# Gathering each block of 256 edges once instead of once for each tile that it touches, in two stages of a graph network on one Trainium2 core

## What is computed

```python
x = x + L0_gnn(layernorm(x), src, dst, ...)         # GIN: sum over neighbours, then a two-layer MLP, batch norm
x = x + L0_ffn(layernorm(x)[None], ...)[0]          # mixture of 16 experts, the best 2 of them
x = x + L1_gnn(layernorm(x), node_vec1, src, dst, edge_attr_4, edge_attr_8, ...)   # tensor-product messages
x = x + L1_ffn(layernorm(x)[None], ...)[0]          # mixture of 8 experts, the best 1
```

```python
neigh = segment_sum(node_feats[src], dst)                       # L0_gnn
h = (1 + eps) * node_feats + neigh
# L1_gnn: y0 (64 values) and y1 (64 x 3) of each node; w_a..w_d (64 each) and ea0, ea1 (1 + 3) of each edge
mid0 = w_a * y0[src] * ea0
mid1 = w_b * einsum('euc,ec->eu', y1[src], ea1) / sqrt(3)
mid2 = (w_c * y0[src])[:, :, None] * ea1[:, None, :]
mid3 = (w_d * ea0)[:, :, None] * y1[src]
agg = segment_sum(concat(mid0, mid1, mid2, mid3), dst)
```

## Time and profile before

| what | us |
|---|---|
| median of three runs | 2367.6 |
| profiled execution, device time | 2366.55 |
| its span | 2364.5 |
| first gather stage, first to last gather issued | 62.7 to 641.7 |
| message stage, first to last gather issued | 1246.1 to 1891.7 |
| granted TensorE clock, mean share | 0.908 |

### The profile page before, as it was taken

How to read it: one execution, slowest core, us unless ns; L and a number is a source line. 1 busy time by engine, 2 the same in 40 slices (tenths; PEclk the granted TensorE clock), 3 DMA queues, 4 the chain that set the end, 5 groups by cost and what they waited for, 6 DMA issues and landing times. The chain is left out here.

```text
span 2364.5 us, 37045 instructions
## 1 busy us (share of the span) xinstructions
PE 1939.7 (82%) x10646; PEld 1596.8 (68%) x10646; DVE 1135.9 (48%) x2491; ACT 1031.6 (44%) x3208; POOL 1152.2 (49%) x1143
## 2 busy tenths in 40 slices
PE   2788888888688767999466988888888878959998
PEld 1555555555356647999345978878778875649997
DVE  5433333333322664444557877777777742141111
ACT  3444444444034402332265766666666626513332
POOL 1777777777600005555107777777777700002221
PEclk7899999999689558999677999999999998959999
DMA  9667676676300118999716766666666604036663
GB/s 237 182 219 223 211 224 222 212 223 211 107 18 0 55 39 293 352 353 343 194 44 198 205 185 194 190 190 189 188 189 190 176 21 92 22 107 200 199 200 98
DMA packets 273478, 413.50 MB, mean 175 GB/s; under 512 B 67662, under 2 KB 162500, under 8 KB 273053
## 3 DMA queue, kind: packets, MB, share of 16 engines
q1 hardware_dynamic: 218056, 258.46, 35.7%
q0 software_dynamic: 54784, 150.16, 21.4%
q10 hardware_dynamic: 462, 2.76, 0.4%
HBM read 324.41 MB, written 87.84 MB: 174 GB/s over the span
## 5 line engine op out<-in xcount | busy, mean ns | idle before, releaser
L1725 POOL DMA_INDIRECT msg_got<-y_dram,pair_src x464 | 505.5, 1090 | 241.8 <-issue 132.5
L1738 ACT ACTIVATE msg_scaled<-msg_plain,msg_w 128x125 f32<-128x125 f32 x1392 | 415.9, 386 | 234.5 <-DVE msg_plain L1774 224.2
L632 POOL DMA_INDIRECT sum_got<-xn_dram,pair_src x464 | 438.9, 946 | 156.1 <-issue 131.6
L673 PEld LDWEIGHTS sum_ps_sum<-sum_got,sum_onehot 128*125 128x125 f32 x928 | 178.9, 200 | 239.7 <-issue 198.7
L673 PE MATMUL sum_ps_sum<-sum_got,sum_onehot 128*125 128x256 f32 x928 | 262.3, 408 | 92.4 <-DMA sum_got<-xn_dram,pair_src 91.9
L1248 ACT ACTIVATE ffn_run_hid<-ffn_run_ps_h,cols 128x128 f32<-128x128 f32 x512 | 145.9, 368 | 391.0 <-PE ffn_run_ps_h L1207 391.0
L1756 PE MATMUL msg_ps_z<-msg_prod,msg_plain 128*125 128x256 f32 x928 | 244.4, 386 | 83.7 <-ACT msg_scaled L1738 41.0
L1765 PEld LDWEIGHTS msg_ps_z<-msg_prod,msg_scaled 128*125 128x125 f32 x2320 | 290.0, 188 | 13.2
L1765 PE MATMUL msg_ps_z<-msg_prod,msg_scaled 128*125 128x128 f32 x2320 | 291.4, 273 | 0.0
L732 DVE TENSOR_TENSOR agg<-sum_ps_sum,agg 125x256 f32 x232 | 98.5, 425 | 373.4 <-PE sum_ps_sum L673 373.4
L703 ACT ACTIVATE sum_wide<-sum_ps_w,sum_rec 128x128 f32<-128x128 f32 x416 | 130.0, 364 | 285.5 <-PE sum_ps_w L659 285.5
(11 more groups left out here) (294 smaller groups left out, 2409.8 us busy)
## 6 DMA issues: line engine op xcount, KB each, us to landing
ffn_run_w<-in_L_ffn_w SPq DMA_DIRECT2D x128, 512.0 KB, 6.6
msg_w<-edge_w SPq DMA_DIRECT2D x232, 260.0 KB
edge_w<-sum_wide SPq DMA_DIRECT2D x52, 1040.0 KB, 4.9
ffn_run_w<-in_L_ffn_Wd SPq DMA_DIRECT2D x32, 1024.0 KB, 5.6
sum_got<-xn_dram,pair_src POOLq DMA_INDIRECT x464, 3.0
msg_got<-y_dram,pair_src POOLq DMA_INDIRECT x464
ffn_rows<-xn SPq DMA_DIRECT2D x10, 560.0 KB
table_got<-ffn_results SPq DMA_DIRECT2D x10, 560.0 KB
```

What stands on the lines that cost most here:

```text
L632: pool.indirect_dma_start(got[:, n % RING, u, :], None, k.xn_dram, bass.IndirectOffsetOnAxis(ap=k.pair_src[:, n, u:u + 1].bitcast(U32), ax ...
L673: last = pe.matmul(ps_sum[n % ZB][0:P, :], onehot[n % OB][:, u, :], got[:, n % RING, u, :], start=(u == 0), stop=(u == KC - 1))
L1725: pool.indirect_dma_start(got[:, s % RS, c, :, :].rearrange("p k v -> p (k v)"), None, k.y_dram, bass.IndirectOffsetOnAxis(ap=k.pair_src[: ...
L1738: last = act.activation(scaled[s % MB][:, x, c, :], plain[s % MB][:, c, :], ACT.Copy, scale=w[:, s % RS, c, D + x:D + x + 1])
```

## The change

`prepare` no longer makes `pair_src` (the src numbers of each pair) and `pair_start`, but `block_src` (those of each block, by a plain transposition) and `pair_need`: the pair's block plus 1. Both stages gather each block once, into a ring of RING = 32 blocks, block b into place (b + 1) % 32. POOL counts the blocks that have arrived in one semaphore, `blocks_in`: LAG = 4 blocks behind the issue, it waits for the block's gathers and increments it. The readers load `pair_need` into a register, wait until `blocks_in` reaches it, and read `got` at the place need % 32. POOL waits, before it issues block b, until the pairs up to b - 8 are done (AHEAD = 32 - 25 = 7). In the message stage the ring of weights has 3 steps instead of 4, the products are made for each pair apart (six instructions of half the size), and the last two of a pair's eight output components are opened by a product of a bf16 row of ones with a bf16 row of zeros instead of by the zeros in `prod`.

```diff
@@ prepare, PE @@
-            for f, w in enumerate((1, 0)):
-                for u in range(KC):
-                    for h, (at, n) in enumerate(HALVES):
-                        last = pe.matmul(ps_two[f][:, u, :], ends_f[h][0:n, :, u, w], chosen[0:n, h, :], start=(h == 0), stop=(h == 1))
-                last.then_inc(field_ready, 1)
+            for h, (at, n) in enumerate(HALVES):
+                for u in range(KC):
+                    last = pe.matmul(ps_block[:, u, at:at + n], ends_f[h][0:n, :, u, 1], k.ident[0:n, 0:n], start=True, stop=True)
+            last.then_inc(blocks_ready, 1)
...
@@ sum_neighbours, POOL @@
-            for n in range(NPAIR):
-                if n >= RING:
-                    pool.wait_ge(summed, n - RING + 1)
+            def arrived(b):
+                pool.wait_ge(got_in[b % RING], (b // RING + 1) * 16 * KC)
+                pool.sem_inc(blocks_in, 1)
+
+            for b in range(NB):
+                if b > AHEAD:
+                    pool.wait_ge(summed, b - AHEAD)
                 for u in range(KC):
                     pool.indirect_dma_start(
-                        got[:, n % RING, u, :], None, k.xn_dram,
+                        got[:, (b + 1) % RING, u, :], None, k.xn_dram,
...
+                if b >= LAG:
+                    arrived(b - LAG)
+            for b in range(NB - LAG, NB):
+                arrived(b)
@@ sum_neighbours, PE @@
+                need = pe.value_load(k.pair_need[0:1, n:n + 1], min_val=1, max_val=NB)
+                pe.wait_ge(blocks_in, need)
                 pe.wait_ge(masked, n + 1)
-                pe.wait_ge(got_in[n % RING], (n // RING + 1) * 16 * KC)
                 for u in range(KC):
-                    last = pe.matmul(ps_sum[n % ZB][0:P, :], onehot[n % OB][:, u, :], got[:, n % RING, u, :],
+                    last = pe.matmul(ps_sum[n % ZB][0:P, :], onehot[n % OB][:, u, :],
+                                     got[:, ds(need % RING, 1), u, :].rearrange("p o d -> p (o d)"),
@@ sum_messages, POOL (the rest as in sum_neighbours) @@
+                if b > AHEAD:
+                    pool.wait_ge(made, (b - AHEAD + 1) // 2)
@@ sum_messages, PE @@
                         pe.matmul(z[0:P, 0:4, :], mask[:, c, :], p[:, c, 0:4, :], start=(u == 0), stop=False)
+                        if u == 0:
+                            pe.matmul(z[0:P, 6:8, :].rearrange("p k v -> p (k v)"), k.ones[0:1, 0:P], zeros[0:1, :], start=False, stop=False)
                     for x in range(3):
                         for u in range(KC):
                             c = KC * h + u
-                            if x == 0 and u == 0:
-                                last = pe.matmul(z[0:P, 4:8, :].rearrange("p (o k) v -> p o k v", o=2), by[:, x, c, :],
-                                                 p[:, c, 4:12, :].rearrange("p (o k) v -> p o k v", o=2)[:, :, 0:4:3, :],
-                                                 start=False, stop=False)
-                            else:
-                                last = pe.matmul(z[0:P, 4:6 + x:1 + x, :], by[:, x, c, :], p[:, c, 4 + x:8:3 - x, :],
-                                                 start=False, stop=(x == 2 and u == KC - 1))
+                            last = pe.matmul(z[0:P, 4:6 + x:1 + x, :], by[:, x, c, :], p[:, c, 4 + x:8:3 - x, :],
+                                             start=False, stop=(x == 2 and u == KC - 1))
@@ sum_messages, DVE @@
+                need = [dve.value_load(k.pair_need[0:1, n:n + 1], min_val=1, max_val=NB) for n in (2 * s, 2 * s + 1)]
                 dve.wait_ge(w_in[s % RS], 32 * (s // RS + 1))
-                dve.wait_ge(got_in[s % RS], 64 * (s // RS + 1))
-                if s >= 2:
-                    dve.wait_ge(summed, s - 1)
-                dve.tensor_tensor(p[:, :, 0:8:7, :], v[:, :, 0:4:3, :], y[:, :, 0:1, :].to_broadcast([128, CH, 2, MUL]), ALU.mult)
...
+                dve.wait_ge(blocks_in, need[1])
+                if s >= XB:
+                    dve.wait_ge(summed, s - XB + 1)
+                for h in range(2):
+                    y = got[:, ds(need[h] % RING, 1), :, :, :].rearrange("p o u k v -> p (o u) k v")
+                    at = slice(KC * h, KC * h + KC)
+                    dve.tensor_tensor(p[:, at, 0:8:7, :], v[:, at, 0:4:3, :], y[:, :, 0:1, :].to_broadcast([128, KC, 2, MUL]), ALU.mult)
+                    for q in (1, 2):
+                        last = dve.tensor_tensor(p[:, at, 3 * q - 2:3 * q + 1, :], v[:, at, q:q + 1, :].to_broadcast([128, KC, 3, MUL]),
+                                                 y[:, :, 1:4, :], ALU.mult)
+                last.then_inc(made, 1)
...
-                dve.memset(prod[b][:, :, 8:12, :], 0.0).then_inc(zeroed, 1)
+            dve.memset(zeros[:, :], 0.0).then_inc(zeros_made, 1)
```

More of the change, by code:

```diff
@@ L386, in _ @@
             last.then_inc(rows_ready, 1)
-            pe.wait_ge(chosen_made, 2)
-            pe.wait_ge(ends_made, 2)
-            for f, w in enumerate((1, 0)):
-                for u in range(KC):
-                    for h, (at, n) in enumerate(HALVES):
-                        last = pe.matmul(ps_two[f][:, u, :], ends_f[h][0:n, :, u, w], chosen[0:n, h, :], start=(h == 0), stop=(h == 1))
-                last.then_inc(field_ready, 1)
+            pe.wait_ge(ends_made, 2)
+            for h, (at, n) in enumerate(HALVES):
+                for u in range(KC):
+                    last = pe.matmul(ps_block[:, u, at:at + n], ends_f[h][0:n, :, u, 1], k.ident[0:n, 0:n], start=True, stop=True)
+            last.then_inc(blocks_ready, 1)
+            pe.wait_ge(chosen_made, 2)
+            for u in range(KC):
+                for h, (at, n) in enumerate(HALVES):
+                    last = pe.matmul(ps_two[1][:, u, :], ends_f[h][0:n, :, u, 0], chosen[0:n, h, :], start=(h == 0), stop=(h == 1))
+            last.then_inc(field_ready, 1)
             pe.wait_ge(loaded, 16 * vec_loads)
@@ L1694, in sum_messages @@
         w = ph.sb("w", [128, RS, CH, WREC])
-        got = ph.sb("got", [128, RS, CH, 4, MUL])
+        got = ph.sb("got", [128, RING, KC, 4, MUL])
         plain = [ph.sb(f"plain{b}", [128, CH, P]) for b in range(MB)]
         scaled = [ph.sb(f"scaled{b}", [128, 3, CH, P]) for b in range(MB)]
-        prod = [ph.sb(f"prod{b}", [128, CH, 12, MUL]) for b in range(2)]
+        prod = [ph.sb(f"prod{b}", [128, CH, 8, MUL]) for b in range(XB)]
         ps_z = [ph.ps(f"z{b}", [128, 8, MUL]) for b in range(ZB)]
+        zeros, zeros_made = ph.sb("zeros", [1, 2 * MUL], BF16), ph.sem("zeros_made")
         ps_lanes, lanes_made = ph.ps("lanes", [128, P]), ph.sem("lanes_made")
-        w_in, got_in = ph.sems("w_in", RS), ph.sems("got_in", RS)
-        masked, scaled_made, made, summed, added, zeroed = (
-            ph.sem(x) for x in ("masked", "scaled_made", "made", "summed", "added", "zeroed"))
+        w_in, got_in, blocks_in = ph.sems("w_in", RS), ph.sems("got_in", RING), ph.sem("blocks_in")
+        masked, scaled_made, made, summed, added = (
+            ph.sem(x) for x in ("masked", "scaled_made", "made", "summed", "added"))
         block = ph.ctx.enter_context(nc.Block())
@@ L1713, in _, with arrived @@
                     n = 2 * s + h
[L1714 removed]
+                    need = sp.value_load(k.pair_need[0:1, n:n + 1], min_val=1, max_val=NB)
                     sp.dma_start(w[:, s % RS, KC * h:KC * h + KC, :].rearrange("p u w -> p (u w)"),
[L1716 removed]
+                                 k.edge_w[ds((need - 1) * SB, SB), :].rearrange("(p u) w -> p (u w)", u=KC)).then_inc(w_in[s % RS], 16)
         @block.gpsimd
         def _(pool):
[L1720 to L1724, removed]
[L1725 to L1727 removed]
+            def arrived(b):
+                pool.wait_ge(got_in[b % RING], (b // RING + 1) * 16 * KC)
+                pool.sem_inc(blocks_in, 1)
+            for b in range(NB):
+                if b > AHEAD:
+                    pool.wait_ge(made, (b - AHEAD + 1) // 2)
+                for u in range(KC):
+                    pool.indirect_dma_start(
+                        got[:, (b + 1) % RING, u, :, :].rearrange("p k v -> p (k v)"), None, k.y_dram,
+                        bass.IndirectOffsetOnAxis(ap=k.block_src[:, b, u:u + 1].bitcast(U32), axis=0)).then_inc(got_in[b % RING], 16)
+                if b >= LAG:
+                    arrived(b - LAG)
+            for b in range(NB - LAG, NB):
+                arrived(b)
         @block.scalar
@@ L1800, in _ @@
             mask(0)
-            for b in range(2):
-                dve.memset(prod[b][:, :, 8:12, :], 0.0).then_inc(zeroed, 1)
+            dve.memset(zeros[:, :], 0.0).then_inc(zeros_made, 1)
             dve.memset(k.agg[:, :, :], 0.0).then_inc(added, 1)
```

36 lines of the change are left out of this document (20 added, 16 removed).

## The result

The changed kernel's median is 2268.96 us (four runs, 2266.26 to 2271.19), and 2366.5 us (four runs, 2364.76 to 2368.01) that of the kernel before beside it: a ratio of 0.9587, with a 95% interval of 0.9572 to 0.9602. The forecast was 2250 us with a range of 2228 to 2294. Sign and range were right, and the middle was 19 us low. The profiled execution took 2271.19 us, 95.4 less than that of before.

The account below looks back on a forecast made before the run. It took POOL to bound both gather stages, with DVE bounding the message stage after the change. 2366.55 less 60 (first stage) and 57 (message stage) gave 2249.6, so 2250 us, range 2228 to 2294.

Parts of the forecast that it names:

- The engine that holds the message stage: Message stage: DVE sets the step at 4.98 us, with PE at 4.58 and POOL at 5.06 at worst.
- First stage, 60.0 from POOL: First gather stage: 48 of 464 gathers go, 1.2505 us each, taking 60.0 us from POOL.
- `LAG` at 0: POOL's added wait and increment cost 0, since its sequencer hands over some twelve gathers ahead.
- Rival (c): POOL's sequencer instruction stands in the gather chain, 17 us in the first stage and 10 in the other: 2275; chance 0.08.
- PE's register load: First gather stage: about 1 us of sequencer a pair, hidden behind 1.73 us of products already queued.
- Rival (d): First gather stage: PE's register load empties its queue, 3.2 us a pair, 134 us slower there: 2444; chance 0.05.
- DVE's step of 4.98: Message stage: 4.35 us plus 0.20 for six products instead of three plus 0.42 of exposed register loads.
- PE's zero product at 0.11: Message stage: the added zero product costs one 128-column instruction, 0.11 us, between bounds of 0.05 and 0.48.
- rival (b): Message stage: DVE's exposure at 0.8 or PE's zero product at 0.48, a step of 5.35 us: 2293; chance 0.12.
- The 4 us kept for the first tile: Message stage: 4 us left for the first tile, where DVE still follows POOL, lowering the gain from 60.7 to 57.
- The signs: If right: 416 gathers a stage, first-stage last at about 582 us, DVE steps of 4.9 to 5.1, POOL idling.
- Rival (a): Message stage: POOL stays the bound with its stretching at 35 to 67 us: 2225 to 2256, middle 2238; chance 0.18.

Follow-up runs that it names:

- loads_early: The changed kernel with DVE's register loads for the next message-stage step moved behind this step's products: 2266.61 us, ratio 0.9574.
- z_bf16_rows128: The changed kernel with the message stage's bf16 zero product over 128 rows instead of one: 2257.68 us, ratio 0.953.
- lag1_first_stage: The changed kernel with LAG = 1 instead of 4 in the first gather stage: 2381.01 us, ratio 1.0064.
- first_stage_only: The kernel before with the changed first gather stage alone, its message stage left as it was: 2308.54 us, ratio 0.9762.
- rows128_early: The changed kernel with the bf16 zero product over 128 rows and DVE's next-step register loads behind the products: 2205.5 us, ratio 0.9329.

## Why the prediction was right, and where its size was off

- **The engine that holds the message stage: wrong.** The forecast had the stage follow DVE at 4.98 us, with PE 0.40 below. In the changed kernel PE is busy without a gap and DVE has slack (loads_early: no gain from taking work off DVE); DVE bounds only once PE's zero product is cheap (z_bf16_rows128). That the time still came out in the range was partly luck: PE's 5.13 happened to lie close above DVE's 4.98.
- **First stage, 60.0 from POOL: right** (59.9). POOL was the bound, 416 gathers 1.25 us apart. What I missed is that a sequencer which waits for the last landing also starts its drain late: 2.8 us. I had written that the stage's end keeps its shape.
- **`LAG` at 0: right**, for the reason given; lag1_first_stage showed the cover by taking it away. Rival (c) falls: "issue" stands at 0.30 us a gather as before.
- **PE's register load: hidden, as taken.** In the loop it runs 305 ns (median), not the 493 of the earlier trace rows, and 44.2 of the 46.3 us that PE waited before these products are put down to gathers. Rival (d) falls.
- **The Trainium skill's floor of about 600 ns** under a register load ("DMA: Bandwidth & Descriptors", "Latency and other measured facts") does not agree here: 305 ns on PE, and the exposed part of DVE's two is 0.31 us (z_bf16_rows128).
- **DVE's step of 4.98: right for DVE**, 5.05 where it bounds (z_bf16_rows128), with the products 0.98 us behind the mask where I had 0.59 + 0.42.
- **PE's zero product at 0.11: the mis-sized term.** It was taken as one 128-column instruction, and measures 0.10 with 128 rows, but 0.39 with its one row. PE's step was thus 5.13 and not 4.58, above DVE's 4.98. The step came out at 5.14: 115 x 0.16 = 18 us. My bounds (0.05 and 0.48) held it, and rival (b) names the place and the sign, a zero product of 0.4 us; I had priced it at its end (a step of 5.35, 2293) and gave it 0.12. Since PE's 4.58 lay only 0.40 under the bound and the term counts twice, anything over 0.31 would have made PE the bound, well inside the two ends.
- **The 4 us kept for the first tile** were hardly needed: 41.6 gained instead of 57 is 15, not 18, less.
- **The signs:** 416 gathers, the last at 582 us, the gap before the products and POOL's idle time came as written. The step of 5.14 is just over the 4.9 to 5.1.
- **Rival (a), POOL the bound: falls.** Its stretching shrank to 12.8 us, less than the 35 to 67 that I left it. That shorter products (0.42 and 0.55 us) let a gather go on sooner is argued, not shown: with the same products it was 7.4 us in z_bf16_rows128 and 22.3 in rows128_early, so how DVE and POOL fall together counts too.

The sum against the profiled execution: forecast 2249.6, plus 15 (PE's zero product, less the first tile), plus 4 (routing stage), plus 3 (drain) is 2271.6; measured 2271.2.

## What to carry to other kernels

When the forecast step of the second engine lies within a doubtful term of the first one's, price that term by the nearest row that is like it in *every* respect, rows of weights included: the row of the one-row product was the nearest, though in fp32 and without neighbours, and I passed it over for a 128-row one. Here a small product between products over 128 rows was cheaper when it was padded to their row count than over one row or 64. And where two edits each give nothing or little, run them together before dropping either: two engines may be holding the same step.

## What the runs showed of the hardware

- A product over one row or 64 rows between products over 128 rows costs 0.39 us (bf16), over 128 rows 0.10; in fp32 over one row 0.60, as it is two instructions. With one or 64 rows PEld sits idle 0.34 us before the load (77.8 us in 232), the load starts no earlier than its product, and the products ahead and behind take 0.10 and 0.11 us more; over 128 rows the load starts 0.21 us before its product. The same break shows between 128 and 32 rows (0.57 us of idle time on PEld), none between 128 and 80 or 72 rows (L396, L1039 of the changed kernel). Under bf16 over 128 rows the change of data type can cost at most the 0.05 us that the products behind it take longer (0.48 for 0.43).
- POOL's drain took 8.56 us where it began after the last landing (the changed kernel, and first_stage_only again); begun under running gathers it ended 8.9 us after the last of them had started. Why it takes 8.56 us stays open.
- POOL's gathers were stretched by 66.6 us in all beside DVE's two-input products of 512 and 768 columns, and by 12.8 with 256 and 384. The Trainium skill ("SBUF — State Buffer", "Who interferes with whom") says that a DVE instruction with two SBUF inputs contends with a GpSimd instruction that reads SBUF. The trace agrees; the size did not follow the products' length alone, as 7.4 and 22.3 us with the same products show (z_bf16_rows128, rows128_early).
- The unchanged routing stage took 138.3 to 145.7 us in the ten kernels, less at a higher granted clock (0.92 and 0.94) than at a lower one (0.88).
